# A fused attention and FFN kernel: turns of q and k moved behind the output product, PSUM banks exchanged

## The reference

```
x = x + attn(cond(x))     # cond: a 32x32 matrix per batch, chosen by a style id
x = x + ffn(cond2(x))     # cond2: a 512x512 matrix per batch, chosen by an adapter id

attn: qkv = clip(h @ w_qkv.T, -8, 8); q, k = layer_norm(q), layer_norm(k)
      scores = q @ k.T / 4 + alibi bias, causal, 32 heads of 16; softmax; @ v; @ w_out.T
ffn:  relu(y @ up)**2 @ down + (y @ fc1 @ expert @ fc2) * (sum of the two best gate logits)
      then layer_norm with gamma and beta
```

## Time and profile before

| | |
|---|---|
| median of 3 runs | 1126.41 us (1125.82 to 1129.65) |
| the profiled execution | 1129.65 us, its span 1127.9 us |
| PE busy | 1083.4 us, 96% of the span |
| POOL, DVE, ACT busy | 713.8, 676.3, 600.6 us (63%, 60%, 53%) |
| mean granted TensorE clock | 0.990 |
| HBM | 93.97 MB read, 42.47 MB written |

### The profile page before, as it was taken

One profiled execution on the slowest core, in us unless ns is written; L12 is line 12 of the kernel. 1 busy time (PEld: TensorE's weight loads), 2 busy tenths in 40 slices (PEclk: granted clock), 3 DMA queues, 4 the chain that ended last, 5 costly groups with the idle time before them and its releaser, 6 DMA issues.

```text
span 1127.9 us, 28302 instructions
## 1 busy us (share of the span) xinstructions
PE 1083.4 (96%) x11396; PEld 876.0 (78%) x11396; DVE 676.3 (60%) x1040; ACT 600.6 (53%) x985; POOL 713.8 (63%) x612
## 2 busy tenths in 40 slices
PE   5999999999999999999989999999999999999994
PEld 3877778788887888788767778787878888787883
DVE  5567667676666667666667245565556565554432
ACT  4466767676766777777767424435261624333220
POOL 4566878788888787878666463556455464433342
PEclk9999999999999999999999999999999999999997
DMA  7125555556554556565567953232414224030101
GB/s 276 41 78 182 183 187 180 169 168 220 173 195 158 198 171 229 170 214 170 175 215 233 350 184 105 84 94 92 126 49 125 67 86 102 28 85 28 47 28 38
DMA packets 95296, 160.84 MB, mean 143 GB/s; under 512 B 46400, under 2 KB 47168, under 8 KB 89792
## 3 DMA queue, kind: packets, MB, share of 16 engines
q1 hardware_dynamic: 79456, 118.16, 32.5%
q0 software_dynamic: 12224, 34.10, 9.5%
q10 hardware_dynamic: 3488, 6.78, 1.7%
HBM read 93.97 MB, written 42.47 MB: 121 GB/s over the span
## 4 chain that ended last, share of the span: by engine, by line
PE 93%; issue 2%; DMA 1%; POOL 1%; DVE 1%; ACT 0%; SPq 0%; POOLq 0%; DVEq 0%; ACTq 0%
PE banks L675 16%; PE banks L860 16%; PE pair L884 15%; PE bank L724 8%; PE bank L675 7%; PE bank L790 7%; PE banks L877 4%; PE bank L877 4%; PE banks L790 3%; PE bank L665 3%; PE pair L692 3%; PE pair L752 2%; PE banks L830 1%; PE banks L735 1%; PE banks L771 1%
## 5 line engine op out<-in xcount | busy, mean ns | idle before, releaser
L1752 POOL TENSOR_TENSOR w_lo<-w2t,w_hi 128x2048 fp32r<-128x2048 f32 x38 | 174.8, 4600 | 39.4 <-ACT w_hi L1053 39.3
L1822 POOL TENSOR_TENSOR u_lo<-act,u_hi 128x512 fp32r<-128x512 f32 x64 | 82.7, 1293 | 102.4 <-ACT u_hi L1253 102.2
L675 PE MATMUL banks<-wqkv_hi,h_hi 128*128 128x512 f32 x256 | 104.7, 409 | 0.2
L860 PE MATMUL banks<-yT_hi,up_hi 128*128 128x512 f32 x256 | 100.8, 394 | 0.0
L675 PE MATMUL banks<-wqkv_hi,h_lo 128*128 128x512 f32 x256 | 100.7, 393 | 0.0
L675 PE MATMUL banks<-wqkv_lo,h_hi 128*128 128x512 f32 x256 | 100.6, 393 | 0.0
L860 PE MATMUL banks<-yT_hi,up_lo 128*128 128x512 f32 x256 | 99.8, 390 | 0.0
L860 PE MATMUL banks<-yT_lo,up_hi 128*128 128x512 f32 x256 | 99.7, 389 | 0.0
L884 PE MATMUL pair<-down_lo,u_hi 128*128 128x512 f32 x256 | 99.6, 389 | 0.0
L884 PE MATMUL pair<-down_hi,u_hi 128*128 128x512 f32 x256 | 99.6, 389 | 0.0
L884 PE MATMUL pair<-down_hi,u_lo 128*128 128x512 f32 x256 | 99.6, 389 | 0.0
(11 more groups left out here) (217 smaller groups left out, 3048.1 us busy)
## 6 DMA issues: line engine op xcount, KB each, us to landing
w2t<-in_w SPq DMA_DIRECT2D x38, 1024.0 KB
vx<-v_hl SPq DMA_DIRECT2D x128, 68.0 KB
x1g<-x_rows SPq DMA_DIRECT2D x32, 256.0 KB, 2.9
kx<-k_hl SPq DMA_DIRECT2D x124, 64.0 KB
x_rows<-x1t SPq DMA_DIRECT2D x31, 256.0 KB, 3.5
ffn_high<-w_high SPq DMA_DIRECT2D x20, 256.0 KB, 3.3
ffn_low<-w_low SPq DMA_DIRECT2D x20, 256.0 KB, 3.4
stage<-in_wqkv SPq DMA_DIRECT2D x3, 1024.0 KB, 8.2
```

Of the source, the lines that this page charges most:

```text
L675: m = e.matmul(into, a[:, c, :], b[:, n, c, :], start=(c == 0 and k == 0), stop=(c == KC - 1 and k == 2))
L860: i = e.matmul((B2, B3)[n % 2], a[:, w, cols], b[m % 2][:, c, :], start=(c == 0 and k == 0), stop=(c == KC - 1 and k == 2))
L1752: e.tensor_tensor(w2_lo[:, :, :], w2t[:, :, :], w2_hi[:, :, :].bitcast(F32), ALU.subtract).then_inc(d_wlo, 1)
L1822: e.tensor_tensor(u_lo[n % FC][:, :], act[n % 2][:, :], u_hi[n % FC][:, :].bitcast(F32), ALU.subtract) \
```

## The change

Five things change, all for tiles with in_halves(t):

- PE calls turn_q(i-1) and turn_k(i-1) behind out_project(i-4), ahead of values(i-3).
- Turned q and k live in banks47, a turned slot and turned values in banks23, where they share with project_q and project_k.
- The chunk's PSUM copy goes from B4 to B6.
- ACT normalizes q and k later in the pass, and scales and rounds them behind soft_exp. It rounds the adapter weights of the next pass (high_w2) after that. Chunks are rounded ahead of the probabilities, planes later.
- DVE makes low_k and low_q of tile i-2 in pass i, behind stats_of of q and ahead of take_k. SP issues spread_k(i-2) behind store_x1 of pass i.

```diff
--- before.py
+++ after.py
...
-    turned_values = banks47[:, :, KC * HALF:2 * KC * HALF]
+    turned_slot = half(banks23, 0)
+    turned_values = banks23[:, :, KC * HALF:2 * KC * HALF]
     def q_at(t):
-        return half(banks23, 0) if in_halves(t) else whole(B7 if t == T - 1 else B3)
+        return half(banks47, 0) if in_halves(t) else whole(B7 if t == T - 1 else B3)
     def k_at(t):
-        return half(banks23, 1) if in_halves(t) else whole(B4 if t < 3 else B5)
+        return half(banks47, 1) if in_halves(t) else whole(B4 if t < 3 else B5)
     def route_bank(c):
...
                     store_route(i - 2)
+                if in_halves(i - 2):
+                    spread_k(i - 2)
                 if 0 <= i - 5 < CHUNKS:
                     keep_chunk(i - 5)
+                if 0 <= i - 4 < CHUNKS:
+                    load_chunk(i - 4)
+                if i >= 5:
+                    load_w2(i - 5)
                 if i >= T - 8:
...
                     load_planes(i - T + 9)
-                if 0 <= i - 4 < CHUNKS:
-                    load_chunk(i - 4)
-                if i >= 5:
-                    load_w2(i - 5)
                 if i == 1:
...
                     spread_v(0)
-                if i >= 1:
+                if i >= 1 and not in_halves(i - 1):
                     spread_k(i - 1)
...
             store_x1(T - 6)
+            spread_k(T - 3)
             upto(e, "x1", T - 6)
...
                 upto(e, "hlo", t - 1)
+                if t > 5:
+                    e.wait_ge(r_low, min(t - 5, CHUNKS))
                 for c in range(KC):
...
             def turn_values(t):
...
                 upto(e, "olo", t - 1)
-                if t:
-                    e.wait_ge(r_low, min(t, CHUNKS))
-                if t + 4 > LAG:
-                    e.wait_ge(d_tl, min(t + 4 - LAG, LAST))
+                if values_halved(t):
+                    upto(e, "ck", t + 4)
+                elif t == T - 5:
+                    upto(e, "qlo", T - 3)
+                    upto(e, "klo", T - 3)
                 for b in range(BPT):
...
                     e.wait_ge(d_tl, s)
-                if s <= LAST:
+                if slot_halved(s):
+                    upto(e, "ck", s + LAG)
                     upto(e, "olo", s + LAG - 5)
-                    e.wait_ge(r_low, min(s + LAG - 4, CHUNKS))
+                elif s == LAST:
+                    upto(e, "qlo", T - 3)
+                    upto(e, "klo", T - 3)
                 for c in range(KC):
...
                             rows = slice(HALF * g, HALF * g + HALF)
-                            m = e.transpose(half(banks47, 0)[:, c, g, :], xg[s % 2][rows, P * c:P * c + P],
+                            m = e.transpose(turned_slot[:, c, g, :], xg[s % 2][rows, P * c:P * c + P],
                                             ident[rows, rows])
...
             def project_q(i):
                 upto(e, "cq", i - 1)
-                if in_halves(i - 2):
-                    upto(e, "qlo", i - 2)
-                    upto(e, "klo", i - 2)
+                if i > LAG:
+                    e.wait_ge(d_tl, i - LAG)
+                    upto(e, "olo", i - 5)
                 project(i, 0, B2, "pq")
             def project_k(i):
...
             def turn_q(t):
-                upto(e, "ck", t + 1)
+                if in_halves(t):
+                    upto(e, "qlo", t - 1)
+                    upto(e, "klo", t - 1)
+                    upto(e, "olo", 1)
+                    e.wait_ge(s_routec, KC)
+                else:
+                    upto(e, "ck", t + 1)
                 turn_qk(t, qn[t % 2], "qn", q_at(t), "tq")
             def turn_k(t):
...
                 if i >= LAG:
-                    turn_slot(i - LAG, banks47)
+                    turn_slot(i - LAG, banks23)
                 if i >= 4:
                     turn_values(i - 4)
-                if i >= 1:
+                if i >= 1 and not in_halves(i - 1):
                     turn_q(i - 1)
...
                     out_project(i - 4)
+                if in_halves(i - 1):
+                    turn_q(i - 1)
+                    turn_k(i - 1)
                 if i >= 3:
...
                     upto(e, "ot", s + LAG - 4)
-                    e.activation(whole(xgT_hi[:, :]), half(banks47, 0), ACT.Copy).then_inc(d_tc, 1)
+                    e.activation(whole(xgT_hi[:, :]), turned_slot, ACT.Copy).then_inc(d_tc, 1)
                 else:
...
             def high_chunk(n):
...
                 e.activation(w_high[:, :], w_raw[:, :], ACT.Copy).then_inc(r_high, 1)
-                upto(e, "olo", n)
-                if n + 5 > LAG:
-                    e.wait_ge(d_tl, n + 5 - LAG)
-                e.activation(B4, w_raw[:, :], ACT.Copy).then_inc(r_bank, 1)
+                upto(e, "x1", n)
+                e.activation(B6, w_raw[:, :], ACT.Copy).then_inc(r_bank, 1)
             def fetch(ready, dst, part, first_, count):
...
             def scale_q(t):
                 upto(e, "tq", t)
-                if in_halves(t):
-                    upto(e, "tk", t)
                 for c in range(KC):
...
                     high_weights(3)
+                if i in (2, 3, 4):
+                    keep_route(i - 1)
+                if 0 <= i - 5 < CHUNKS:
+                    high_chunk(i - 5)
                 if i >= 3:
                     high_probs(i - 3)
-                if i in (2, 3, 4):
-                    keep_route(i - 1)
                 if i == 2:
...
                     e.activation(gate_hl[:, :, 0, :], gate_raw[:, :, :], ACT.Copy).then_inc(m_ghi, 1)
-                if 0 <= i - 5 < CHUNKS:
-                    high_chunk(i - 5)
-                if i >= T - 8:
-                    join_planes(i - T + 8)
-                    high_planes(i - T + 8)
-                if i >= LAG:
-                    high_w2(i - LAG)
-                if i >= 1:
+                if i == LAG:
+                    high_w2(0)
+                if i >= 1 and not in_halves(i - 1):
                     normalize(i - 1)
                 if i >= LAG:
-                    slot_in(i - LAG, banks47)
+                    slot_in(i - LAG, banks23)
                 if i >= 4:
...
                     high_h(i + 1)
-                if i >= 1:
+                if i >= T - 8:
+                    join_planes(i - T + 8)
+                    high_planes(i - T + 8)
+                if in_halves(i - 1):
+                    normalize(i - 1)
+                elif i >= 1:
                     scale_q(i - 1)
...
                     soft_exp(i - 2)
+                if in_halves(i - 1):
+                    scale_k(i - 1)
+                    scale_q(i - 1)
+                    high_k(i - 1, k_hl)
+                    high_q(i - 1)
+                    high_w2(i + 1 - LAG)
             def relu(n):
...
             high_planes(EARLY_GROUPS * KC - 1)
-            high_w2(LAST)
             e.wait_ge(r_kept, 32 * CHUNKS)
...
             def low_chunk(n):
...
                 e.wait_ge(r_bank, n + 1)
-                e.tensor_tensor(w_low[:, :], B4, w_high[:, :].bitcast(F32), ALU.subtract).then_inc(r_low, 1)
+                e.tensor_tensor(w_low[:, :], B6, w_high[:, :].bitcast(F32), ALU.subtract).then_inc(r_low, 1)
             def low_slot(s, bank_):
...
                     upto(e, "ohi", s + LAG - 4)
-                    e.tensor_tensor(whole(lo), half(banks47, 0), whole(hi), ALU.subtract).then_inc(d_tl, 1)
+                    e.tensor_tensor(whole(lo), turned_slot, whole(hi), ALU.subtract).then_inc(d_tl, 1)
                 else:
...
             def low_q(t):
                 upto(e, "qhi", t)
-                if in_halves(t):
-                    upto(e, "khi", t)
                 upto(e, "s", t - 1)
...
             def low_k(t, dst):
                 upto(e, "khi", t)
+                if in_halves(t):
+                    upto(e, "qhi", t)
                 if t < T - 1:
...
                 stats_of(i, 0, qn, "cq")
-                if 0 <= i - 5 < CHUNKS:
-                    low_chunk(i - 5)
-                if i >= T - 8:
-                    low_planes(i - T + 8)
+                if in_halves(i - 2):
+                    low_k(i - 2, k_hl)
+                    low_q(i - 2)
                 take_k(i)
...
                 aggregate(i)
+                if 0 <= i - 5 < CHUNKS:
+                    low_chunk(i - 5)
                 take_v(i)
...
                 if i >= LAG:
-                    low_slot(i - LAG, banks47)
+                    low_slot(i - LAG, banks23)
                 if i >= 4:
...
                     bias_max(i - 2)
-                if i >= 1:
+                if i >= 1 and not in_halves(i - 1):
                     low_q(i - 1)
                     low_k(i - 1, k_hl)
+                if i >= T - 8:
+                    low_planes(i - T + 8)
                 if i >= 4:
...
             stats_of(T - 1, 0, qn, "cq")
+            low_k(T - 3, k_hl)
+            low_q(T - 3)
             low_planes(EARLY_GROUPS * KC - 1)
...
```

## The result

The changed kernel takes 1241.28 us in the median of 4 runs (1238.62 to 1246.45), the kernel before beside it 1126.12. The ratio is 1.103 with a 95% interval of 1.098 to 1.108: slower, as forecast, and inside the range of 1200 to 1250. The likeliest value, 1234, was 7 us too low. The profiled execution has a span of 1241.2 us.

What follows compares the result with a forecast made beforehand. The prediction took PE to bound the kernel, at 93% of the chain. Stalls 72.5, clock 32.3 and turns 2.5 sum to 107.3 us, which on the median of 1126.41 gives 1234 us, range 1200 to 1250.

Steps and rivals of the forecast that it cites:

- The wait of project_k on q_lo: In passes 7 to 31 PE finishes project_q, then waits for four DVE operations before project_k: 25 stalls.
- Its price: project_k starts 2.90 us later in each of 25 passes, with nothing to cover it: 72.5 us.
- The clock: PE's clock falls behind 19 of the 25 stalls, three quarters, at 1.7 us each: 32.3 us.
- The turns: turn_q and turn_k behind out_project add one change of kind of work, 0.1 us in 25 passes: 2.5 us.
- Rival 4: Faster: fewer transposes ahead of scores remove late-instruction idle times and clock falls, about 12 us, giving 1114; chance 0.02.
- The rest: ACT's later scaling, slot weights, SP's spread of k and the PSUM homes add no further cost.
- these spare times: Margins before PE would wait: 2.4 us for the spread of k at scores, 4 us for slot weights at adapt_slot.
- The sum: Stalls 72.5, clock 32.3 and turns 2.5 make 107.3 us more than before; the forecast itself had chance 0.75.

Runs made afterwards that it cites:

- e1: The changed kernel without project_k's wait on q_hi and q_lo of tile i-2 where in_halves(i-2): 1145.94 us, ratio to before 1.016.
- e3: The changed kernel, its wait kept, with DVE making low_q ahead of low_k: 1216.92 us, ratio to before 1.0791.
- e4: e3 with DVE's stats_of of q moved behind low_q and low_k: 1184.07 us, ratio to before 1.0515.
- e6: e1 with the turns of q and k, and ACT's normalize for them, at their old places: 1128.89 us, ratio to before 1.0021.
- e7: e1 with the planes' loads, joins and stores at their old places on SP, ACT and DVE: 1145.00 us, ratio to before 1.0147.
- e5: e1 with turn_q and turn_k ahead of out_project instead of behind it: 1149.16 us, ratio to before 1.0189.
- e10: e6 with DVE making the planes' last low part after take_v, behind the loop, instead of ahead of take_k: 1131.51 us, ratio to before 1.0032.
- e9: The kernel before with 16 more small matmuls (64 instructions in the trace) ahead of everything: 1122.93 us, ratio to before 0.9959.

## Why the prediction was right, and what it missed

**The wait of project_k on q_lo: right.** e1, e3 and e4 show it: taken away, the stall goes; with one or two operations fewer in front of q_lo it shrinks by what they take.

**Its price, 2.90 us x 25 = 72.5: 4% low.** project_k starts 362.42 - 359.18 = 3.24 behind project_q's last matmul, where the step would be 0.22: 3.02 us late, 75.5 in all. The term that was off is the pick-up behind DVE's result: 0.06 in the earlier trace rows, 362.42 - 362.21 = 0.21 here.

**The clock, 32.3 us: right in size, the count by luck.** 17 of the 25 stalls were followed by a fall, against the 19 that I chose from three cases, but two of the 17 lasted 6.83 us instead of 3.41: 64.8 us at half clock, which is 32.4 us. Three more falls came behind other idle times (2.62, 1.92 and 4.76 us), and the three of the kernel before have gone. For the whole execution, what a lowered clock takes is (1 - mean clock) x span: 0.010 x 1127.9 = 11.3 before and 0.036 x 1241.2 = 44.7 after, 33.4 more. The prediction held that no idle time over 2 us had been without a fall, which is so for the stage that it looked at; near its start the kernel before has one of 2.32 us (it ends at 24.56) with clock 1.00 behind it. The rule of the Trainium skill ("TensorE: Matmul & The Clock Gate", Part 1) that the activity monitor runs free of the kernel fits: stalls of one length, 2.86 us, had both outcomes.

**The turns, 2.5 us: right for the pass, but not the whole.** In an undisturbed pass the new place costs 0.14 us, 3.5 in all (e1 against e6), where 0.1 and 2.5 were forecast for one more change of kind. It does not show against the kernel before, because the rest of the change gives 0.11 us a pass back (18.19 in e6, 18.30 before). But the place of the turns costs 17 us in e1, mostly through instructions that come late, and that the prediction did not have. Rival 4 saw the mechanism and had the sign wrong: I supposed that half the transposes less ahead of scores would help, and put up to 8 us given back into the low end of the range. In the changed kernel the "issue" idle times over 0.5 us from 100 us on, without the 25 stalls, are 16.5 us against 11.1 before.

**The rest, nothing: nearly right.** e6 gives 0.2%. In the changed kernel PE waits neither for kx nor for w_lo. Without the stall two of these spare times run out: e1 waits 3.3 us for kx and 2.1 us for w_lo, so the stall hid them, as the prediction said for kx.

**The sum.** 75.5 + 33.4 = 108.9 of the 113.3 us between the two spans. Two smaller terms make up the rest. A pass of 21.44 us is 0.13 longer than 18.29 + 3.02, some 3 us in 25 passes. And PE's idle time without the 25 stalls is 47.9 us (119.6 - 71.7) against 44.5 before, 3.4 more. All four make about 2 us too much, as some falls began inside an idle time and took nothing there. The longest of the other idle times is this one:

```profile
614.52 0.76 PE L681 MATMUL banks<-wqkv_hi,h_hi 128*128 128x512 f32 x1 [4.76 <-issue]
```

It begins at 609.76, with no wait in the program open. SP had just issued transposing loads of planes, and the DMA queue in that stretch was full:

```profile
607.13 2.56 SPq L529 DMA_TRANSPOSE planes<-y_rows  x2
```

```profile
q1 hardware_dynamic: 1664, 2.04, 99.9%
```

The fetch of the instruction block began at 611.63, 2.1 us after PE had run out, and PE's next instruction came 2.67 us later, as behind the other fetches. So not the fetch itself was slow, but its start was late. That the full queue delayed the start is possible, and e7 points that way (there it was 0.9 us late), but it is not shown.

**Why the turns' place brings late instructions: half open.** That the fetches begin late is shown by the packets. Where this happens is known, and why is not. The block ends with idle time lie 146 to 216 instructions behind the last transpose in before (transposes end at 149 of the 606, the ends at 295 to 365), and ends elsewhere cost nothing, apart from one in pass 30. Of the eight ends in that stretch two, at 313 and 329, cost nothing either. In e1 there are two groups of transposes in a pass, ending at 112 and 410, and idle times lie 173 to 215 behind either. In e5 the second group ends at 386, and they lie 119 to 223 behind it. So one place became two, and the moved turns made the end of values such a place. What it is about the transposes, or about waits in front of them, that makes a fetch begin late some 200 instructions later, no run here tells. The Trainium skill, page "Runtime: NRT & Kernel Launch", section "Instruction fetch mechanics", has blocks of 256 instructions, which the table bears out, and calls the crossing mostly hidden; here most crossings are, but some leave PE idle for 1 to 2.5 us, and the longest for 4.8 us.

## What to carry to other kernels

When an operation is moved behind another in one engine's queue, look for every wait on its result in the other queues, also in lines that the diff leaves alone: two lines that had cost nothing made 95 of 115 us here. A stall on TensorE costs more than itself where the clock falls behind it: shortening 25 of them from 2.86 to 1.54 us took out 32 us of idle time (the waits of project went from 77.5 to 45.6 us) and saved 57. Where an engine executes some ten thousand small instructions, late instructions move the time with their order and even with their number: 64 more changed it by 0.4% here, and 10 of the 17 us that the turns' place costs are idle time of this kind. Compare variants with that in mind.

## What the runs showed of the hardware

- In three kernels with different orders 20 of 21 idle times over 0.9 us with the releaser "issue" fall on the same place in blocks of 256 PE instructions (193 to 196). PE goes on 2.15 to 2.72 us after the fetch of the block began; where it began at least 2.1 us ahead of the end of the block before, PE has no idle time over 0.25 us. 64 instructions more ahead of the loop moved the idle times to other passes and made the kernel 0.4% faster.
- The profile gave project_k's wait for DVE's q_lo the releaser "issue" in all 25 cases, and in e10 also a wait that ended with ACT's normalized k. Six waits of e4 were named, by ACT's q_hi.
- The length of an idle time alone does not decide whether the clock falls. None fell behind 1.92 and 2.21 us in e1, or behind 3.01 us in e9 (it ends at 612.49); one fell behind 1.79 us in e9. The rows of e1 behind 1.92 and 2.21, and of e9 behind 3.01 and 1.79:

```profile
220.30:224.00 3.70, 3.70 (x22) 2.99 (x22) 1.60 (x4) 3.70 (x6) 2.04 (x3) 1.00 0.44 118
432.20:436.00 3.80, 3.80 (x27) 3.13 (x22) 1.76 (x4) 3.80 (x6) 2.17 (x3) 1.00 0.45 124
```

```profile
612.60:616.00 3.40, 3.40 (x18) 2.82 (x18) 1.38 (x2) 1.54 (x2) 0.99 (x1) 1.00 1.12 315
...
245.60:249.00 3.40, 3.40 (x10) 2.63 (x9) 3.15 (x5) 0.87 (x2) 2.48 (x2) 0.51 0.34 108
```
